# A retention layer's order of work on TensorE and ScalarE: the carried state goes next to the scores, the gate behind the increment, the turning ahead of the output, the output's sum into a gate bank

## The chip, the cores and the metric

The kernel runs on one core of a Trainium2 chip. The metric is the device time of one execution in microseconds. TensorE (PE), VectorE (DVE), ScalarE (ACT) and GpSimd (POOL) each work through a list of instructions of their own, in order, and wait for each other on semaphores. The results of matmuls land in eight PSUM banks of 128 x 512 floats, which DVE and ACT empty.

## What is computed

Two transformer layers on x of 2 x 1024 x 128. Layer 0 is a retention with 8 heads (keys of 64, values of 128), then a feed-forward part that holds a causal attention with 16 heads of 8 and a mixture of four experts. Layer 1 is a full attention with 16 heads and a ternary linear map. The retention, on which the change bears most:

```
q, k = rotary(x Wq), rotary(x Wk);  v = x Wv;  g = x Wg
scores[t, s] = (q_t . k_s) / 8 * gamma_h ** (t - s)   for s <= t
o = groupnorm(scores v) * gn_weight + gn_bias
x = layernorm(x + (o * silu(g)) Wo)
```

## The kernel before

**The retention** (the first quarter of the span) goes over 16 tiles of 128 tokens, 8 for each sequence. In a sequence it runs chunk by chunk: scores inside a tile, and a state of 8 x 64 x 128 that is carried from tile to tile. Everything is in fp32. TensorE's loop over n holds, in this order of issue: the transposes of the turned q and k of tile n (lines 684 and 686, into banks 6 and 7, a wait on `rot_ready` ahead of them), the projection of q and k of tile n+1 (L654, banks 0 and 1), the values of tile n (L705, banks 2 and 3), the scores (L716, banks 4 and 5, which need `qkT_copied` and `onT_affine`), the gate of tile n-1 (`gate_product`, L485, banks 0 and 1, which needs `rot_muls` of tile n+1), the increment of the state (L742, bank 6, needs `v_copied`), the carried state against q (L754, accumulated in banks 2 and 3), the output of the scores (L759, needs `sc_masked`), the projection of tile n-2's gated output (`project_out`, L495, bank 7) and the turning of tile n-1's normed output (`turn_normed`, L504, banks 4 and 5).

Bank 7 has a further use: in tiles 7 to 14 two short pieces a tile of the next stage (latent, q, k, values of the causal attention) pass through it (`use_bank7`, slot 0 ahead of the scores, slot 1 behind the gate; lines 632 to 647).

**ScalarE** in a tile: keeps and squares the output of tile n-1 (`keep_output`, L511 and L514), copies the transposed q and k (L948), applies the group norm's weight and bias to tile n-2 in eight instructions (`affine`, L521), copies the values (L954), opens the gate (`open_gate`, L529). **VectorE**: sums the squares (L535), multiplies for the rotary turn (L786, L787, L789; the last counts `rot_muls`), gates (L542), masks the scores (L812), normalises (L548), adds the state (L826), adds the output to x and takes its statistics (`add_output`, L554 to L557). At the end of tiles 5, 9 and 13 it works out a root and scales four tiles for the next stage (L836, L372 to L376, L440). **GpSimd**: decays the state (L872), works out the root of the group norm (`group_root`, L563, L383 to L387), at tiles 6 and 10 a second root of the same kind (`norm1_rooted`, L432 to L434 and L383 to L387), and turns and scales q and k of tile n+1 (L889, L890, L894; the last counts `rot_ready`).

After tile 15 TensorE goes on along a list that `order()` writes: the gate of tile 15 (D16a), the outputs of tiles 14 and 15 (D16b, D17a) and the first scans. VectorE splits q and k of the second half of sequence 0 (L577) behind the output of tile 13; SyncE stores the parts, loads them back as stacks, and TensorE's first scan (L1519) waits for these.

**The attention of layer 0** has 96 units of 128 keys in 16 blocks. In step s TensorE computes scores (S, L1599 and L1608, two halves x of two heads), scans for a later block's maxima (A, L1519, emptied by VectorE in L1972), and the values of unit s-1 (V, L1634). ScalarE takes the exponentials (L1792), and at the last V of a block it copies the sums out (L1805). In a narrow unit (at most 256 queries) V's half 0 holds no matmul and half 1 holds them all. The lines that set where V stands:

```
for x in range(2):
    if (s, x) in score_use:
        seq.append(("S", (s, x)))
    seq += pairs[...]
    if 0 < s <= NU:
        seq.append(("V", (s - 1, x)))
```

## Time and profile before

| what | value |
|---|---|
| time, median of 3 runs | 996.72 us (996.59 to 1000.06) |
| the profiled execution's own time | 996.77 us |
| its span, first to last instruction | 995.0 us |
| PE busy | 878.4 us (88%) |
| DVE busy | 763.1 us (77%) |
| ACT busy | 654.6 us (66%) |
| POOL busy | 390.0 us (39%) |
| mean granted clock of TensorE | 0.971 |
| chain that ended last | PE 52%, DVE 29%, ACT 7% |

The profile comes from one execution. Starts are in microseconds from the first instruction. A matmul's end is modelled; what a group of matmuls takes is better read as the distance from its start to the start of the group behind it. "T0" below is the start of the q and k transposes of a tile (L684).

### The profile page before, as it was taken

What the parts mean: (1) busy time and instruction counts of PE and PEld (TensorE: products, weight loads), DVE (VectorE), ACT (ScalarE), POOL (GpSimd) and SP (SyncE); (2) the same over time, 40 slices, a digit from 0 to 9 for tenths busy, and PEclk for the clock granted to TensorE, in tenths of its full rate; (3) what the DMA queues carried; (4) which work ended last, traced back from release to release, by engine and by line L of the source; (5) the groups of instructions that cost most, each with busy time, mean ns of one, the idle gap of its engine ahead of it and who ended that gap; (6) DMA issues with size and microseconds to landing.
All of it is one profiled execution on the core that took longest, in us unless ns stands there. A gap on an engine that the chain in (4) does not pass through costs nothing.

```text
span 995.0 us, 22895 instructions
## 1 busy us (share of the span) xinstructions
PE 878.4 (88%) x9093; PEld 446.3 (45%) x9098; DVE 763.1 (77%) x1156; ACT 654.6 (66%) x1285; POOL 390.0 (39%) x607
## 2 busy tenths in 40 slices
PE   8999999998877889888988778889989999999983
PEld 5777777777632443333663222336322222222232
DVE  4677675856587788887567498886889999999845
ACT  3555565655525778785556548765778888998981
POOL 3764767778332652135354111442441111111330
PEclk9999999999899999998998899999999999999995
DMA  8000000200501044111420611033106000100000
GB/s 302 1 2 1 1 2 1 75 1 1 153 1 42 22 132 141 39 41 57 140 63 22 185 23 40 8 111 94 50 13 193 21 20 21 39 2 3 5 22 22
DMA packets 49406, 52.53 MB, mean 53 GB/s; under 512 B 8874, under 2 KB 40618, under 8 KB 49140
## 3 DMA queue, kind: packets, MB, share of 16 engines
q1 hardware_dynamic: 45012, 48.12, 15.9%
q0 software_dynamic: 4288, 2.94, 1.1%
q8 instruction: 73, 1.20, 0.5%
q14 instruction: 33, 0.27, 0.1%
HBM read 32.37 MB, written 19.68 MB: 52 GB/s over the span
## 4 chain that ended last, share of the span: by engine, by line
PE 52%; DVE 29%; ACT 7%; issue 6%; DMA 3%; POOL 2%; SPq 1%; DVEq 0%; ACTq 0%; POOLq 0%
DVE arena L1972 20%; PE banks L1634 11%; PE banks L1599 7%; PE banks L1519 5%; ACT arena L1792 3%; PE banks L759 3%; PE banks L485 3%; PE banks L495 2%; PE banks L1709 2%; PE banks L1717 2%; PE banks L654 1%; PE banks L754 1%; PE banks L716 1%; PE banks L705 1%; ACT arena L521 1%
## 5 line engine op out<-in xcount | busy, mean ns | idle before, releaser
L1792 ACT ACTIVATE arena<-banks 128x512 f32<-128x512 f32 (+1 forms) x768 | 409.3, 587 | 109.2 <-PE banks L1599 78.0
L1972 DVE TENSOR_REDUCE arena<-banks 128x2 f32<-128x1024 f32 (+1 forms) x384 | 439.8, 1197 | 51.9 <-PE banks L1519 27.6
L1634 PE MATMUL banks<-arena 128*9 128x256 f32 (+1 forms) x3328 | 252.1, 378 | 6.7 <-ACT arena L1805 4.6
L1519 PE MATMUL banks<-arena 56*128 56x512 bf16 (+3 forms) x896 | 162.3, 364 | 34.2 <-DVE arena L1972 27.2
L1599 PE MATMUL banks<-arena 61*128 61x512 bf16 (+4 forms) x896 | 164.8, 367 | 26.7 <-ACT arena L1792 21.5
L1599 PEld LDWEIGHTS banks<-arena 61*128 61x128 bf16 (+1 forms) x896 | 44.5, 93 | 183.2 <-ACT arena L1792 155.1
L1376 POOL CAST arena<-arena 16x128 bf16<-16x128 f32 x32 | 8.9, 280 | 293.0 <-ACT arena L1860 289.0
L1634 PEld LDWEIGHTS banks<-arena 128*9 128x9 f32 x3328 | 51.4, 88 | 128.7 <-issue 80.5
L1519 PEld LDWEIGHTS banks<-arena 56*128 56x128 bf16 x896 | 45.0, 95 | 60.7 <-DVE arena L1972 47.8
L383 POOL TENSOR_TENSOR arena<-arena 128x8 f32<-128x8 f32 (+1 forms) x35 | 51.3, 1466 | 30.3 <-DVE arena L2136 27.9
L1386 POOL DMA_DIRECT2D arena<-arena x96 | 55.1, 577 | 10.7 <-POOL arena L1379 9.2
L521 ACT ACTIVATE arena<-banks,arena 128x128 f32<-128x128 f32 x128 | 46.4, 477 | 0.5 <-PE banks L504 0.5
L511 ACT ACTIVATE arena<-banks 128x1024 f32<-128x1024 f32 x16 | 16.4, 1022 | 39.8 <-PE banks L759 39.8
L1969 DVE TENSOR_REDUCE arena<-banks 128x4 f32<-128x1024 f32 (+1 forms) x32 | 30.5, 956 | 14.3 <-PE banks L1529 13.3
L1416 POOL DMA_INDIRECT expert_rows<-arena x22 | 21.3, 970 | 50.9 <-DVE arena L2068 50.6
L554 DVE TENSOR_TENSOR arena<-banks,arena 128x128 f32<-128x128 f32 x16 | 4.6, 290 | 47.0 <-PE banks L495 47.0
L529 ACT ACTIVATE arena<-banks 128x1024 f32<-128x1024 f32 x16 | 16.4, 1026 | 34.2 <-PE banks L485 32.8
L485 PE MATMUL banks<-arena 128*128 128x128 f32 x256 | 34.3, 290 | 2.9 <-DVE arena L789 2.9
L1788 ACT ACTIVATE arena<-banks 128x512 f32<-128x512 f32 (+1 forms) x64 | 27.9, 489 | 13.0 <-PE banks L1608 12.7
L485 PEld LDWEIGHTS banks<-arena 128*128 128x128 f32 x256 | 31.4, 200 | 5.0 <-DVE arena L789 3.0
L759 PE MATMUL banks<-arena 128*128 128x128 f32 x256 | 32.8, 280 | 0.3 <-DVE arena L812 0.3
L495 PE MATMUL banks<-arena 128*128 128x128 f32 x256 | 32.3, 280 | 0.7 <-DVE arena L542 0.7
(243 smaller groups left out, 1442.7 us busy)
## 6 DMA issues: line engine op xcount, KB each, us to landing
arena<-k_products SPq DMA_DIRECT2D x32, 224.0 KB
arena<-q_products SPq DMA_DIRECT2D x64, 112.0 KB
q_products<-arena SPq DMA_DIRECT2D x16, 384.0 KB, 3.4
k_products<-arena SPq DMA_DIRECT2D x16, 384.0 KB, 3.8
arena<-e_w SPq DMA_DIRECT2D x22, 256.0 KB, 3.4
arena<-arena POOLq DMA_DIRECT2D x96, 4.0 KB, 1.8
sorted_rows<-c_pads SPq DMA_DIRECT2D x2, 709.5 KB, 9.3
arena<-sorted_rows SPq DMA_DIRECT2D x4, 258.0 KB, 3.2
```

What stands on the lines that cost most here:

```text
L383: link(eng.tensor_tensor(y, v, epst[:, 1:2].to_broadcast(list(v.shape)), ALU.pow))
L485: ins = nc.tensor.matmul(bank(s // 4)[:, (s % 4) * P:(s % 4 + 1) * P], wg[:, s * P:(s + 1) * P], XT[:, i, :], start=True, stop=True)
L495: ins = nc.tensor.matmul(bank(7)[:, 0:P], uu[:, s, :], wo[:, s, :], start=(s == 0), stop=(s == RH - 1))
L521: ins = nc.scalar.activation(ga[:, s, :], bank(4 + s // 4)[:, (s % 4) * P:(s % 4 + 1) * P], ACT.Identity, scale=gn[:, 0, s:s + 1], bias=gn ...
L759: ins = nc.tensor.matmul(bank(2 + s // 4)[:, (s % 4) * P:(s % 4 + 1) * P], sm[:, s, :], vv[n % 2][:, s, :], start=first, stop=True, skip_g ...
L1386: g_.dma_start(rows, nmp[k % 2][:, i, :]).then_inc(mrow[k % 2], 16)
L1519: ins = nc.tensor.matmul(bank(first + par)[:, at:at + hi - lo], Qs[k_][rows, qc, y, qo:qo + P], Ks[k_][rows, y, lo:hi], start=True, stop=n ...
L1599: ins = nc.tensor.matmul(bank(S_BANK + (use + par) % SCORES)[:, at:at + C - o], Ks[n % NS][rows, y, kt * P:(kt + 1) * P], Qs[n % NS][rows, ...
L1634: ins = nc.tensor.matmul(PS[h * VROWS:h * VROWS + VW, AV_BANK, o:end], V[:, b, kt, HG * g + h, :], Pr[u % PROBS][:, h, o:end], start=(kt = ...
L1792: s_.activation(Pr[s % PROBS][:, 2 * x + par, o:C], scores[:, o:C], ACT.Exp) \
L1969: v_.tensor_reduce(of, two_banks.rearrange("p r (y e) -> p r y e", y=2)[:, :, :, 0:width], AX.X, ALU.max).then_inc(ring_dve, 1)
L1972: v_.tensor_reduce(of[:, :, x], two_banks[:, :, 0:width], AX.X, ALU.max).then_inc(ring_dve, 1)
```

## The change

In the retention, on TensorE: the carried state (L754) moves from behind the increment to right behind the scores, together with the wait on `v_copied`; the increment (L742) follows; the gate (L485) moves behind the increment; the turning (L504) goes ahead of the projection of the output (L495). The sum of that projection is placed in bank 0 for tiles 0 to 13 and in bank 7 for 14 and 15. With this the transposes wait for bank 7's last reader and no longer for `y_added`, the projection of q and k waits for `y_added`, and `project_out` waits for the gate's silu of the tile before (`g_silu`). ScalarE applies the affine (L521) ahead of the copy of the transposed q and k (L948). In `order()` both halves of V follow the first half of the step if the unit is narrow. In D16a the gate of tile 15 waits for `y_added` of tile 13.

```diff
--- before.py
+++ after.py
@@ -486,13 +486,19 @@
                                        wg[:, s * P:(s + 1) * P], XT[:, i, :], start=True, stop=True)
             ins.then_inc(g_done, 1)
 
+        def y_bank(i):
+            return 0 if i < NTILE - 2 else 7
+
         def project_out(pe, i):
 
             pe.wait_ge(u_ready, i + 1)
             ready(pe, y_added, i)
-            ready(pe, use_emptied, sum(at <= (i + 2, 1) for at in USES))
+            if i < NTILE - 2:
+                pe.wait_ge(g_silu, i + 2)
+            else:
+                ready(pe, use_emptied, len(USES))
             for s in range(RH):
-                ins = nc.tensor.matmul(bank(7)[:, 0:P], uu[:, s, :], wo[:, s, :],
+                ins = nc.tensor.matmul(bank(y_bank(i))[:, 0:P], uu[:, s, :], wo[:, s, :],
                                        start=(s == 0), stop=(s == RH - 1))
             ins.then_inc(y_done, 1)
 
@@ -551,7 +557,7 @@
 
             v_ = nc.vector
             dve.wait_ge(y_done, i + 1)
-            v_.tensor_tensor(X[:, i, :], bank(7)[:, 0:P], X[:, i, :], ALU.add).then_inc(y_added, 1)
+            v_.tensor_tensor(X[:, i, :], bank(y_bank(i))[:, 0:P], X[:, i, :], ALU.add).then_inc(y_added, 1)
             dve.wait_ge(y_added, i + 1)
             link(v_.bn_stats(stats[:, i, :], X[:, i, :]))
             link(v_.bn_aggr(mv[:, i, :], stats[:, i, :]))
@@ -678,7 +684,7 @@
                 if this:
 
                     pe.wait_ge(rot_ready, n + 1)
-                    ready(pe, y_added, n - 2)
+                    ready(pe, use_emptied, sum(at <= (n - 1, 1) for at in USES))
                     ready(pe, state_ready, n)
                     for p4 in range(4):
                         nc.tensor.transpose(bank(6)[:, p4 * P:(p4 + 1) * P], qd[n % 2][:, p4 * P:(p4 + 1) * P], ident)
@@ -689,6 +695,7 @@
                 if n + 1 < NTILE and n != 0:
 
                     ready(pe, g_silu, n - 1)
+                    ready(pe, y_added, n - 2)
                     project_qk(n + 1)
                 if n == -1:
 
@@ -716,21 +723,16 @@
                             ins = nc.tensor.matmul(bank(4 + par)[:, p4 * P:(p4 + 1) * P], qkT[rows, 4 + p4, :],
                                                    qkT[rows, p4, :], start=True, stop=True)
                     ins.then_inc(sc_done, 1)
-                i = n - 1
-                if 0 <= i < NTILE:
-
-
-                    if n == 1:
-                        pe.wait_ge(load["gv"], 32)
-                    if n + 1 < NTILE:
-                        pe.wait_ge(rot_muls, n + 2)
-                    else:
-                        pe.wait_ge(g_silu, i)
-                    gate_product(pe, i)
-                use_bank7(n, 1)
+                    pe.wait_ge(v_copied, n + 1)
+                    ready(pe, state_ready, n)
+                    if not first:
+                        for p4 in range(4):
+                            for par in range(2):
+                                rows = slice(par * RD, (par + 1) * RD)
+                                nc.tensor.matmul(bank(2 + par)[:, p4 * P:(p4 + 1) * P], qkT[rows, p4, :],
+                                                 state[(n - 1) % 2][rows, p4 * P:(p4 + 1) * P],
+                                                 start=(p4 == 0), stop=False, skip_group_check=True)
                 if this:
-
-                    pe.wait_ge(v_copied, n + 1)
                     if last:
 
                         nc.tensor.matmul(bank(6)[:, 0:P], ident, ident, start=True, stop=True).then_inc(delta_done, 1)
@@ -744,25 +746,29 @@
                                     kd[n % 2][:, (2 * p4 + par) * RD:(2 * p4 + par + 1) * RD],
                                     vv[n % 2][:, 4 * par + p4, :], start=True, stop=True)
                         ins.then_inc(delta_done, 1)
+                i = n - 1
+                if 0 <= i < NTILE:
+
+
+                    if n == 1:
+                        pe.wait_ge(load["gv"], 32)
+                    if n + 1 < NTILE:
+                        pe.wait_ge(rot_muls, n + 2)
+                    else:
+                        pe.wait_ge(g_silu, i)
+                        pe.wait_ge(y_added, n - 2)
+                    gate_product(pe, i)
+                use_bank7(n, 1)
                 if this:
-
-                    ready(pe, state_ready, n)
-                    if not first:
-                        for p4 in range(4):
-                            for par in range(2):
-                                rows = slice(par * RD, (par + 1) * RD)
-                                nc.tensor.matmul(bank(2 + par)[:, p4 * P:(p4 + 1) * P], qkT[rows, p4, :],
-                                                 state[(n - 1) % 2][rows, p4 * P:(p4 + 1) * P],
-                                                 start=(p4 == 0), stop=False, skip_group_check=True)
                     pe.wait_ge(sc_masked, n + 1)
                     for s in range(RH):
                         ins = nc.tensor.matmul(bank(2 + s // 4)[:, (s % 4) * P:(s % 4 + 1) * P], sm[:, s, :],
                                                vv[n % 2][:, s, :], start=first, stop=True, skip_group_check=not first)
                     ins.then_inc(o_done, 1)
+                if n >= 1:
+                    turn_normed(pe, n - 1)
                 if n >= 2:
                     project_out(pe, n - 2)
-                if n >= 1:
-                    turn_normed(pe, n - 1)
 
         @block.vector
         def _(dve):
@@ -942,12 +948,12 @@
             for n in range(NTILE):
                 if n >= 1:
                     keep_output(act, n - 1)
+                if n >= 2:
+                    affine(act, n - 2)
                 if n < NTILE:
                     act.wait_ge(qkT_done, n + 1)
                     ready(act, o_done, n)
                     s_.activation(qkT.rearrange("p s t -> p (s t)"), pair(3), ACT.Copy).then_inc(qkT_copied, 1)
-                if n >= 2:
-                    affine(act, n - 2)
                 if n < NTILE:
                     act.wait_ge(v_done, n + 1)
                     ready(act, o_done, n - 1)
@@ -1147,7 +1153,8 @@
                     if -6 <= s < 0:
                         seq.append(("warm", 2))
                     if 0 < s <= NU:
-                        seq.append(("V", (s - 1, x)))
+                        late = narrow(*us[s - 1])
+                        seq += [("V", (s - 1, y)) for y in range(2) if (0 if late else y) == x]
                     if x == 0:
                         seq += midst.get(s, [])
                 seq += sorted(after.get(s, []), key=lambda e: (e[0] != "put") + (e[0] == "split"))
@@ -1482,6 +1489,7 @@
                             pe.wait_ge(o_kept if q >= 2 else g_silu, NTILE)
                     if kind == "D16a":
                         pe.wait_ge(g_silu, k)
+                        pe.wait_ge(y_added, k - 1)
                         gate_product(pe, k)
                     elif kind == "D16b":
                         project_out(pe, k - 1)
```

## Rows read from the trace of the kernel before

**Rows 1.** Timeline, tiles 3 and 4: start, us, engine, line, form, count, [idle]

```profile
55.31 1.16 PE L716 MATMUL banks<-arena 64*128 64x128 f32 x16 [0.56 <-ACT arena L521]
56.40 2.05 PE L485 MATMUL banks<-arena 128*128 128x128 f32 x16
...
60.51 2.05 PE L759 MATMUL banks<-arena 128*128 128x128 f32 x16
62.40 1.95 PE L495 MATMUL banks<-arena 128*128 128x128 f32 x16
64.18 1.04 PE L504 MATMUL banks<-arena 128*128 128x128 f32 x8
65.06 0.60 PE L684 MATMUL banks<-arena 128*128 128x128 f32 x4
...
65.93 1.89 PE L654 MATMUL banks<-arena 128*128 128x512 f32 x4
...
67.65 1.88 PE L705 MATMUL banks<-arena 128*128 128x512 f32 x4
...
70.10 1.16 PE L716 MATMUL banks<-arena 64*128 64x128 f32 x16 [0.56 <-ACT arena L521]
...
62.60 1.03 ACT L511 ACTIVATE arena<-banks 128x1024 f32<-128x1024 f32 x1 [3.05 <-PE banks L759]
63.65 1.06 ACT L514 ACTIVATE arena<-arena 128x1024 f32<-128x1024 f32 x1
...
67.05 2.90 ACT L521 ACTIVATE arena<-banks,arena 128x128 f32<-128x128 f32 x8
...
69.79 1.08 ACT L954 ACTIVATE arena<-banks 128x1024 f32<-128x1024 f32 x1
```

**Rows 2.** Timeline, TensorE, the gate of tile 0 in tile 1

```profile
28.39 2.02 PE L485 MATMUL banks<-arena 128*128 128x128 f32 x16 [0.47 <-DVE arena L789]
```

**Rows 3.** Timeline, tile 6: output added, root on GpSimd, tile 7's transposes

```profile
93.96 0.29 DVE L554 TENSOR_TENSOR arena<-banks,arena 128x128 f32<-128x128 f32 x1 [2.38 <-PE banks L495]
...
99.34 0.20 POOL L563 TENSOR_SCALAR arena<-arena 128x8 f32<-128x8 f32 x1 [6.41 <-DVE arena L535]
...
110.03 1.04 POOL L894 TENSOR_TENSOR arena<-arena 128x512 f32<-128x512 f32 x1
...
111.12 0.66 PE L684 MATMUL banks<-arena 128*128 128x128 f32 x4 [0.68 <-POOL arena L894]
```

**Rows 4.** Timeline, end of tile 10: GpSimd's last turn, tile 11's transposes

```profile
172.32 1.04 POOL L894 TENSOR_TENSOR arena<-arena 128x512 f32<-128x512 f32 x1
...
173.65 0.60 PE L684 MATMUL banks<-arena 128*128 128x128 f32 x4
```

**Rows 5.** Timeline, tiles 14 and 15 and the first scan

```profile
228.24 2.05 PE L485 MATMUL banks<-arena 128*128 128x128 f32 x16 [0.83 <-DVE arena L789]
...
237.98 0.60 PE L684 MATMUL banks<-arena 128*128 128x128 f32 x4
...
243.02 1.16 PE L716 MATMUL banks<-arena 64*128 64x128 f32 x16 [2.28 <-ACT arena L521]
...
253.77 1.29 DVE L577 TENSOR_TENSOR arena<-arena 128x512 bf16<-128x512 f32 x2
...
266.71 0.39 PE L1519 MATMUL banks<-arena 56*128 56x512 bf16 x2 [2.06 <-DMA arena<-q_products]
```

**Rows 6.** Stages: length, busy time per engine, granted clock, DMA share, GB/s

```profile
244.00:246.00 2.00, 2.00 (x13) 1.89 (x10) 1.95 (x3) 0.82 (x2) 1.75 (x5) 0.53 0.03 8
246.00:248.00 2.00, 2.00 (x13) 1.88 (x12) 1.18 (x2) 0.18 (x1) 1.47 (x5) 0.62 0.00 0
```

**Rows 7.** Timeline of layer 0's attention, the first step of a block

```profile
401.22 0.39 PE L1599 MATMUL banks<-arena 59*128 59x512 bf16 x2 [0.60 <-ACT arena L1792]
...
401.76 0.41 PE L1634 MATMUL banks<-arena 128*9 128x128 f32 x8
...
402.60 0.61 ACT L1805 ACTIVATE arena<-banks 128x512 f32<-128x512 f32 x1
```

## The prediction

> **What bounds the kernel now.** I read the page's slices first, then the timeline of one plain tile, then the chain that ended last for the places where it leaves TensorE. In the retention TensorE is the bound, and its instructions follow each other with few holes; the reader should look for the holes. A group's length is the distance to the next start. In tile 3 [rows 1] scores take 1.09 (55.31 to 56.40), gate, increment and carried state together 4.11 (to 60.51), the output of the scores 1.89, the projected output 1.78, the turning 0.88, the transposes of q and k 0.87, the projection of q and k 1.72 (65.93 to 67.65); the values, the same shape, another 1.72, to 69.37. Yet the scores start at 70.10. The sum is 14.06, the period 14.79, the hole 0.73 (the row prints 0.56, since ends are modelled). It waits for the affine on ScalarE, which runs 67.05 to 69.95. Tiles 3, 4, 5 and 6 start their scores behind the same hole. In tiles 7 to 14 a piece of the next stage fills it. The other holes: gates that wait for the rotary products (0.47 in tile 1 [rows 2], 0.83 in tile 14 [rows 5]), tile 7's transposes that wait for GpSimd [rows 3], and tile 15, where no projection stands behind the transposes and the hole is 2.28 [rows 5].
>
> **The plain tile after the change.** Count from the start of the transposes, T0. Three lags come from the rows: a consumer starts 0.20 behind the start of the group that follows its producer (62.60 against 62.40), TensorE starts 0.15 behind the end of what it waited for (69.95 to 70.10), and the kept output and its squares take 2.11 (62.60 to 64.71) [rows 1]. The output of the scores now ends at -2.66, ahead of turning and projection. ScalarE keeps it from -2.46 to -0.35, and runs the affine at once, for the turning was done at -1.78: to 2.57. The copy of q and k, taken as long as the values' copy (1.08), ends at 3.65, and TensorE could start the scores at 3.80, while it arrives at 4.31. So that hole is closed, with 0.5 to spare. What is late next is the copy of the values: produced at 4.31, read from 4.51 to 5.59, TensorE may go on at 5.74, but the scores end at 5.40. The gate stood here and hid this; now the carried state waits 0.34. Behind it in TensorE's queue stands all the rest of the tile. I take the whole 0.34; the other bound is a wait of 0.2, if the copy starts TensorE as quickly as the gate of VectorE does. Gain a tile 0.73 - 0.34 = 0.39, for tiles 3, 4 and 5: **1.2**. Moving gate and increment costs nothing here, the sum is the same and the mask is made beside them.
>
> **Tiles 1 and 2.** The wait for the rotary products in tile 1 (0.47 [rows 2]) falls behind carried state and increment; some 0.1 of a wait for the values stays: +0.4. In tile 2 no projected output stands between the scores' output and T0, so ScalarE is late for both orders: 0, between -0.3 and +0.3.
>
> **The output behind the turning is later by a turning.** y is complete 0.88 later against T0: VectorE's `add_output` starts at T0 + 0.20 and no longer at T0 - 0.68. In a plain tile nobody cares. In tile 6 it heads the longest chain of the stage: add (93.96, so T0 is 94.64), root and scaling of four tiles, sum of squares, GpSimd's two roots from 99.34, the turn of q and k to 111.07, tile 7's transposes at 111.12 [rows 3]. This chain takes 17.16 from add to transposes and holds no TensorE work. After the change T0 of tile 7 is 0.20 + 17.16 = 17.36 behind T0 of tile 6; before it was 16.48. **Loss 0.9.** In tile 10 the same chain ended at 173.36 and TensorE came at 173.65 [rows 4], a slack of 0.24 with the lag of 0.05 seen in tile 7: **loss 0.88 - 0.24 = 0.6.** The adds of tile 5's and 9's last step can't hide it: TensorE's own work in tile 6 comes to at most 15.5, so it stands idle 1.9 ahead of T0 of tile 7. Tile 14 has no second root; its gate's 0.83 goes and nothing is late in its place: **gain 0.8.** In the other tiles the order of equal parts changes and the hole isn't there: 0, between -0.3 and +0.3 in all.
>
> **Tile 15.** Before: T0 at 237.98, scores at 243.02, L577 at 253.77 [rows 5], 15.79 behind T0. In these 15.79 the granted clock fell from 2.4 to 1.2 GHz after the hole: 0.53 and 0.62 of full in two stretches of 2 us [rows 6], which is 2 x 0.47 + 2 x 0.38 = 1.7 us of work lost. After: transposes and values to 2.59; the copy of q and k lets the scores start at 3.80 (a hole of 1.2); scores and carried state 2.2, an identity product in the increment's place 0.3, the gate 2.0: 8.3; output of the scores 1.9, turning 0.9, projected output 1.8: 12.9; add at 13.1, its statistics 0.87 as before: L577 at about 13.9. **Gain 1.9**, of which the late output took 0.9. From L577 the way goes over SyncE and DMAs to the first scan at 266.71, which waited for them 2.06 [rows 5]; nothing of the change lies in it. TensorE's other work there has that 2 us of slack against 0.4 us in which it now starts later relative to L577, and the gate of tile 15, which waits 0.6 for the add of tile 13, has the same cover. So what L577 gains the scans gain.
>
> **The clock.** The new idle 1.9 ahead of tile 7 is a new risk. Holes of 0.6 to 0.8 left the clock at 2.4 GHz all through the stage; 2.28 was followed by 1.2 GHz [rows 5, 6]. 1.9 is nearer to the second, and VectorE's mask already holds TensorE about 1 us before it. I take one fall, at the price above: **loss 1.7**, between 0 and 3.4 (tile 11's transposes wait 1.4 as well). The Trainium skill, "TensorE: Matmul & The Clock Gate", section "Part 4: PE-mode transpose", says that a transpose doesn't count as busy for that gate; by this the 0.87 of transposes behind each wait counts as idle too, and both tiles would lose the clock. The trace of before neither shows nor denies it.
>
> **Layer 0's narrow values.** A narrow unit's values move only where something stood between the halves. That is the last unit of a block, sixteen times: its V (0.41, rows 7) passes ahead of the second half's scores, its A, and a block's end. Exponentials wait there at present: TensorE stood 0.60 for ScalarE before the second scores [rows 7], and V now fills that. Up to 0.41 a block, 6.6 in all, if TensorE sets the pace after it, but VectorE's scans or ScalarE do in most steps, and ScalarE has the same instructions: its copy out (0.61) only goes ahead of two exponentials. I take a gain of **0.5**, between -3 and +4.
>
> **Sum.** 1.2 + 0.4 - 0.9 - 0.6 + 0.8 + 1.9 = 2.8 in the retention, less 1.7 for the clock, plus 0.5: 1.6 off the profiled execution's 996.77 (span 995.0, with 1.8 around it), which is within 0.1 of the median. **995.2 us.**
>
> **Rivals.**
> - *The clock holds.* For it: 1.9 us is shorter than any hole after which it fell. 996.8 - 2.8 - 0.5 = 993.5. If V's move is worth 3 more in bubbles, 990.5.
> - *Both of GpSimd's waits cost the clock,* tiles 7 and 11: 996.8 - 2.8 + 3.4 - 0.5 = 996.9. For it the rule on transposes, which the sentence above names; against it 1.4 us of idle is much shorter than 2.28.
> - *Slower: the copy out blocks ScalarE.* It now stands ahead of the second half's exponentials and waits for V, which stands behind the first scan, and so behind VectorE. If VectorE is late there, ScalarE stands with scores ready. Price: the copy's 0.61 once more in each of 16 blocks, 9.8, against the 1.1 that is left: 1005. It decides where ScalarE is the bound and VectorE behind. Against it: the second scores stood behind the same scan before, and the copy had to be over before the next block's V anyway.
> - *The copy of values isn't hidden in more tiles than thought,* or the sum in bank 0 makes the projection wait for the add: 0.28 us of slack in a plain tile. 0.3 in ten tiles would be 3: 998.
>
> **How the numbers follow.** Forecast 0.38; clock holds 0.27; both clocks 0.13; more waits 0.09; slower by the copy 0.07; a large gain in layer 0 0.06. A measurement can tell about 0.5% (5 us). Faster by that, below 991.8, needs the clock and layer 0 together: 0.18. Slower, above 1001.7, needs the copy or several of the waits: 0.09. Same 0.73. Range 989.5 to 1000.0.
>
> **What would show it.** Right: plain tiles 14.4 apart; no wait of L716 for L521, and one of about 0.3 of L754 for L954; T0 of tile 7 17.4 behind T0 of tile 6 with GpSimd as releaser; L577 13.9 behind T0 of tile 15, and TensorE at full clock between. Wrong: a period of 14.06 or over 14.8; tile 7 on time; L1805 with idle time ahead of it on ScalarE in each block; the granted clock at half in tiles other than 7. The prediction fails above all if the falls of the clock in the attention, whose places move with every microsecond, change in number.

## The result and the profile after

The changed kernel takes 990.4 us (median of 8 runs, 987.9 to 992.4) where the kernel before takes 996.7 in the same rounds (8 runs, 994.1 to 1000.1): a ratio of 0.9923, 95% interval 0.9903 to 0.9943. In later rounds, beside the experiments, it was 992.5 against 997.4, ratio 0.9947 (0.9923 to 0.9970). So it is faster by 5 to 6 us. The forecast was 995.2, a gain of 1.6: the time lies inside the range of 989.5 to 1000.0, but the gain is some four times what the sum gave, and it is the "faster, below 991.8" to which the prediction gave 0.18.

The profiled execution took 990.96 us, its span is 989.2 (before: 995.0). From here on "T0" is the start of the transposes of q and k (L690 now, L684 before), and a tile's length is the distance to the next T0. Lines have moved: scores are L723, carried state L732, increment L744, output of the scores L765, projected output L501, turning L510, affine L527, copy of q and k L956, copy of the values L960.

| stretch | before, us | after, us | difference | forecast |
|---|---|---|---|---|
| start to T0 of tile 1 | 22.35 | 22.15 | -0.20 | 0 |
| tiles 1 and 2 | 27.92 | 26.84 | -1.08 | -0.4 |
| tiles 3, 4 and 5, together | 44.36 | 42.16 | -2.20 | -1.2 |
| tile 6 | 16.49 | 17.37 | +0.88 | +0.9 |
| tiles 7, 8 and 9 | 45.55 | 44.37 | -1.18 | 0, and +1.7 for the clock |
| tile 10 | 16.98 | 17.83 | +0.85 | +0.6 |
| tiles 11, 12 and 13 | 47.34 | 46.78 | -0.56 | 0 |
| tile 14 | 16.99 | 15.93 | -1.06 | -0.8 |
| T0 of tile 15 to the first scan | 28.73 | 26.32 | -2.41 | -1.9 |
| first scan at | 266.71 | 259.75 | -6.96 | -1.1 |
| first scan to the end of the span | 728.3 | 729.45 | +1.2 | -0.5 |

Timeline of the kernel after, tile 3 on TensorE and ScalarE (start, us, engine, line, form, count, idle before), the lines that answer to [rows 1]:

```profile
51.59 1.88 PE L712 MATMUL banks<-arena 128*128 128x512 f32 x4
53.40 1.16 PE L723 MATMUL banks<-arena 64*128 64x128 f32 x16
54.59 1.16 PE L732 MATMUL banks<-arena 64*128 64x128 f32 x16
55.68 1.10 PE L744 MATMUL banks<-arena 128*64 128x128 f32 x16
56.71 2.05 PE L485 MATMUL banks<-arena 128*128 128x128 f32 x16
58.60 1.95 PE L765 MATMUL banks<-arena 128*128 128x128 f32 x16
60.38 1.04 PE L510 MATMUL banks<-arena 128*128 128x128 f32 x8
61.26 1.95 PE L501 MATMUL banks<-arena 128*128 128x128 f32 x16
63.05 0.60 PE L690 MATMUL banks<-arena 128*128 128x128 f32 x4
...
48.55 2.88 ACT L527 ACTIVATE arena<-banks,arena 128x128 f32<-128x128 f32 x8
51.28 1.06 ACT L956 ACTIVATE arena<-banks 128x1024 f32<-128x1024 f32 x1
53.51 1.02 ACT L960 ACTIVATE arena<-banks 128x1024 f32<-128x1024 f32 x1 [1.16 <-PE banks L712]
```

The scores stand right behind the values (51.59 to 53.40) and no longer behind a hole: the copy of q and k ends at 52.34, a microsecond ahead of them. The carried state starts at 54.59, 0.06 behind the end of the copy of the values (53.51 + 1.02), so it does wait for it, though no idle time is printed.

Timeline of the kernel after, tiles 6 and 10: the add of the output and the transposes at the other end of the chain, the lines that answer to [rows 3] and [rows 4]:

```profile
91.35 0.29 DVE L560 TENSOR_TENSOR arena<-banks,arena 128x128 f32<-128x128 f32 x1 [2.47 <-PE banks L501]
...
108.52 0.66 PE L690 MATMUL banks<-arena 128*128 128x128 f32 x4 [1.78 <-POOL arena L900]
...
170.72 0.66 PE L690 MATMUL banks<-arena 128*128 128x128 f32 x4 [1.72 <-POOL arena L900]
```

From add to transposes it is 108.52 - 91.35 = 17.17 us in tile 6, and TensorE stands idle 1.78 and 1.72 us ahead of tiles 7 and 11.

Timeline of the kernel after, tile 15 and the first scan, the lines that answer to [rows 5] (SPq is SyncE's queue of transfers), and the stretches behind T0 of tiles 7 and 15 (length, busy time per engine, granted clock, DMA share, GB/s), which answer to [rows 6]:

```profile
233.43 0.60 PE L690 MATMUL banks<-arena 128*128 128x128 f32 x4
...
236.84 1.16 PE L723 MATMUL banks<-arena 64*128 64x128 f32 x16 [0.65 <-ACT arena L956]
...
246.97 1.29 DVE L583 TENSOR_TENSOR arena<-arena 128x512 bf16<-128x512 f32 x2
...
254.68 0.78 SPq L1248 DMA_DIRECT2D arena<-k_products  x2
...
259.75 0.39 PE L1527 MATMUL banks<-arena 56*128 56x512 bf16 x2 [1.35 <-DMA arena<-q_products]
...
108.00:110.00 2.00, 1.48 (x10) 1.24 (x11) 1.22 (x1) 2.00 (x6) 1.88 (x3) 1.00 0.00 0
...
244.00:246.00 2.00, 2.00 (x19) 1.87 (x17) 0.00 (x0) 1.97 (x3) 1.67 (x5) 1.00 0.02 4
```

The granted clock is 1.00 (2.4 GHz) in every such stretch, behind both waits for GpSimd as in tile 15. VectorE's part splitting L583 (the L577 of before) stands 13.54 behind T0 of tile 15, where it stood 15.79.

### The profile page after: what moved, and what is told of

Its sections match the earlier page's. It is cut to its first block, busy times and chain, and to the rows that moved or that the text cites. A ratio compares the mean times of both kernels' runs of the same rounds, so it can differ in the third digit from the quotient of the medians.

```text
span 989.2 us, 22910 instructions
## 1 busy us (share of the span) xinstructions
PE 877.2 (89%) x9098; PEld 440.9 (45%) x9098; DVE 764.4 (77%) x1156; ACT 652.9 (66%) x1285; POOL 390.4 (39%) x607
## 4 chain that ended last, share of the span: by engine, by line
PE 41%; DVE 27%; POOL 12%; issue 9%; ACT 6%; DMA 3%; SPq 2%; DVEq 0%; POOLq 0%; ACTq 0%
DVE arena L1980 19%; PE banks L1642 11%; PE banks L1607 7%; PE banks L1527 5%; ACT arena L1800 4%; POOL arena L383 2%; PE banks L1717 2%; PE banks L1725 2%; DMA arena<-arena 1%; PE banks L660 1%; POOL arena L896 1%; POOL arena L895 1%; PE banks L501 1%; PE banks L765 1%; POOL arena L386 1%
## 5 line engine op out<-in xcount | busy, mean ns | idle before, releaser
L1642 PE MATMUL banks<-arena 128*9 128x256 f32 (+1 forms) x3328 | 254.8, 382 | 5.8 <-ACT arena L1813 3.9
L535 ACT ACTIVATE arena<-banks 128x1024 f32<-128x1024 f32 x16 | 16.4, 1024 | 56.9 <-PE banks L485 55.5
L527 ACT ACTIVATE arena<-banks,arena 128x128 f32<-128x128 f32 x128 | 46.1, 466 | 0.0
L501 PE MATMUL banks<-arena 128*128 128x128 f32 x256 | 31.4, 275 | 2.0 <-DVE arena L548 2.0
L485 PE MATMUL banks<-arena 128*128 128x128 f32 x256 | 32.6, 281 | 0.6 <-DVE arena L560 0.5
L765 PE MATMUL banks<-arena 128*128 128x128 f32 x256 | 31.9, 277 | 1.2 <-DVE arena L818 1.2
L765 PEld LDWEIGHTS banks<-arena 128*128 128x128 f32 x256 | 30.0, 191 | 4.4 <-issue 2.5
L501 PEld LDWEIGHTS banks<-arena 128*128 128x128 f32 x256 | 29.8, 191 | 3.0 <-DVE arena L548 3.0
```

Of the source, the lines that this page charges most:

```text
L485: ins = nc.tensor.matmul(bank(s // 4)[:, (s % 4) * P:(s % 4 + 1) * P], wg[:, s * P:(s + 1) * P], XT[:, i, :], start=True, stop=True)
L501: ins = nc.tensor.matmul(bank(y_bank(i))[:, 0:P], uu[:, s, :], wo[:, s, :], start=(s == 0), stop=(s == RH - 1))
L527: ins = nc.scalar.activation(ga[:, s, :], bank(4 + s // 4)[:, (s % 4) * P:(s % 4 + 1) * P], ACT.Identity, scale=gn[:, 0, s:s + 1], bias=gn ...
L765: ins = nc.tensor.matmul(bank(2 + s // 4)[:, (s % 4) * P:(s % 4 + 1) * P], sm[:, s, :], vv[n % 2][:, s, :], start=first, stop=True, skip_g ...
L1642: ins = nc.tensor.matmul(PS[h * VROWS:h * VROWS + VW, AV_BANK, o:end], V[:, b, kt, HG * g + h, :], Pr[u % PROBS][:, h, o:end], start=(kt = ...
```

## Experiments

"Before" and "after" name the two kernels. Times are medians with the ratio to before and its 95% interval, measured in the same rounds.

### The two parts apart

`e1_values_only` is before with the new order of V alone, `e2_retention_only` is after with the old one:

```diff
-                        late = narrow(*us[s - 1])
-                        seq += [("V", (s - 1, y)) for y in range(2) if (0 if late else y) == x]
+                        seq.append(("V", (s - 1, x)))
```

> The kernel before with layer 0's narrow values alone moved (the order of work in the attention), the retention as it was. The two whole kernels stand 0.77% apart; the traces put 7.0 us of it ahead of the first scan. Theory 1 (the retention holds all of it, the values are worth the 0.5 us of the prediction): ratio 0.9995, between 0.998 and 1.001. Rival (the values fill TensorE's bubbles at each block's end and carry 2 us or more): 0.998 or below. Rival (the copy out blocks ScalarE): above 1.002.

> The changed kernel with the attention's order put back: only the retention's edits. Theory 1: the first scan starts at 259.8 as in the changed kernel, ratio about 0.993. If the values carried 2 us or more, the ratio is 0.995 or above.

Measured: e1 997.2 us, ratio 0.9985 (0.9964 to 1.0007); e2 992.6 us, ratio 0.9929 (0.9900 to 0.9958). The whole gain that can be measured is the retention's. Its tiles in e2 are those of after within 0.03 us, and its first scan stands at T0 of tile 15 + 26.57.

What V's order does is seen in layer 0's first block. Timeline of e1, ScalarE, the exponentials (L1793), the copy out (L1806) and the copy behind it (L1861):

```profile
306.22 0.61 ACT L1806 ACTIVATE arena<-banks 128x512 f32<-128x512 f32 x1
306.69 1.11 ACT L1793 ACTIVATE arena<-banks 128x512 f32<-128x512 f32 x2
307.65 0.25 ACT L1861 ACTIVATE arena<-banks 16x128 f32<-16x128 f32 x1
```

In before the copy out stands at 307.82 and L1860, which is this kernel's L1861, at 308.30. So the copy out is 1.6 earlier, but 1.0 of that is only its new place ahead of two exponentials; the work itself is 0.65 earlier. By L1860/L1861 the lead grows to 0.84 at 343, 1.05 at 375, 1.38 at 421 and 1.9 at 464: some 0.1 to 0.2 a block, no idle time ahead of the copy. So the slower rival (the copy out blocks ScalarE) is out. By the copy that starts at 641.66 in e1 and 646.21 in before the lead is 4.6 in these two profiles, but e1's is its fastest run; between e2 and after at the same place it is nothing (640.66 and 640.72), though e2's first scan is 0.9 later. Two runs further down, e10 and e8, ask the same of whole times once more.

### The turning behind the output again

`e3_output_first` is after with the projected output ahead of the turning, its sum still in bank 0:

```diff
+                if n >= 2:
+                    project_out(pe, n - 2)
                 if n >= 1:
                     turn_normed(pe, n - 1)
-                if n >= 2:
-                    project_out(pe, n - 2)
```

> The changed kernel with the projected output again ahead of the turning, its sum still in bank 0. Theory (the output behind the turning is late by one turning, 0.88 us, at the head of the chains of tiles 6, 10 and 15): the transposes of tile 7 come 16.5 behind those of tile 6 (17.37 in the changed kernel), those of tile 11 16.9 to 17.0 behind those of tile 10 (17.83), the first scan 0.9 earlier against the transposes of tile 15; plain tiles stay at 14.05, since the affine has 0.5 us to spare. In all 2.6 us less than the changed kernel, ratio 0.990 to 0.991. Rival (the affine, now started by a turning that is 1.79 later, holds the scores again): plain tiles at 14.3 to 14.8 and no gain over the changed kernel.

Measured: 987.5 us, ratio 0.9877 (0.9843 to 0.9911). Plain tiles stay at 14.05, tile 6 takes 16.51, tile 10 17.15. So the late output costs what the prediction put on it, 0.86 and 0.68, and gives nothing back: closing the hole doesn't need it. Timeline of e3, part splitting, the first load of a stack and the first scan:

```profile
245.30 1.29 DVE L583 TENSOR_TENSOR arena<-arena 128x512 bf16<-128x512 f32 x2
...
253.01 0.78 SPq L1248 DMA_DIRECT2D arena<-k_products  x2
...
259.89 0.39 PE L1527 MATMUL banks<-arena 56*128 56x512 bf16 x2 [3.70 <-DMA arena<-q_products]
```

L583 comes 12.83 behind T0 of tile 15 (after: 13.54), and the load starts 7.71 behind it in both. But the loads then took 6.88 us to the scan, where after's took 5.07: the scan stands no earlier than in after in this profile.

### ScalarE's old order

`e4_copy_first` is after with ScalarE's copy of q and k ahead of the affine, as in before:

```diff
                 if n >= 1:
                     keep_output(act, n - 1)
-                if n >= 2:
-                    affine(act, n - 2)
                 if n < NTILE:
                     act.wait_ge(qkT_done, n + 1)
...
+                if n >= 2:
+                    affine(act, n - 2)
```

> The changed kernel with ScalarE's copy of the transposed q and k again ahead of the affine. Theory (the hole before the scores was ScalarE's order alone, and the turning's place would not have closed it): the scores of tiles 3 to 6 wait for the affine again, 0.6 to 0.75 a tile, plain tiles at 14.6 to 14.8, tile 15's scores wait over 2 us and the clock falls to half behind it; the gain before the first scan shrinks from 7.0 to 1 to 3 us. Rival (the earlier turning lets the affine start early enough in any order): plain tiles at 14.05.

Measured: 993.3 us, ratio 0.9942 (0.9917 to 0.9967), and its first scan is at 265.18; 2.1 of the 5.4 by which that is later than after's lie in a later start and a longer tile 0, ahead of all that the edit touches. Timeline of e4, tile 5 on TensorE, from its T0 to the next, and the scores of tile 15:

```profile
79.89 0.60 PE L690 MATMUL banks<-arena 128*128 128x128 f32 x4
...
84.92 1.16 PE L723 MATMUL banks<-arena 64*128 64x128 f32 x16 [0.55 <-ACT arena L527]
85.88 1.09 PE L732 MATMUL banks<-arena 64*128 64x128 f32 x16
...
94.27 0.60 PE L690 MATMUL banks<-arena 128*128 128x128 f32 x4
...
241.38 1.16 PE L723 MATMUL banks<-arena 64*128 64x128 f32 x16 [2.27 <-ACT arena L527]
```

The hole is back (0.55, as in [rows 1]), yet a plain tile takes 14.38, not 14.6 to 14.8. The scores start 5.03 behind T0, as before; the 9.35 from there to the next T0 were 9.75 in before (55.31 to 65.06, [rows 1]). The difference of 0.4 is TensorE's own order. In after the same stretch takes 9.65 (53.40 to 63.05), though TensorE's order is that of e4: so the wait for the copy of the values, which is over in time in e4, costs after 0.30. Of this 0.23 shows in the scores (1.19 against 0.96) and the rest in the carried state behind them. In tile 15 the wait for the affine is back too (2.27), the clock falls to half behind it, and L583 stands 16.24 behind T0 where after has 13.54. So of what after gained up to L583, ScalarE's order holds the larger part: 1.7 us between T0 of tile 0 and T0 of tile 15, and 2.7 behind it.

### The length of the wait and the clock

`e5_longer_wait` is after with three products more on GpSimd ahead of the root of tile 6:

```diff
                         pool.wait_ge(n1_scaled, m + 1)
+                        if m == 0:
+                            for _ in range(3):
+                                link(g_.tensor_tensor(sq, ident, ident, ALU.mult))
                         norm1_rooted(link, m).then_inc(n1_rooted, 1)
```

> The changed kernel with three products more on GpSimd (128x128 each) ahead of its root in tile 6, so that TensorE's wait ahead of tile 7's transposes grows from 1.78 us to about 2.8; the rest is the same. Theory A (the length of the idle time decides whether TensorE's clock falls: 1.78 left it at full, 2.06 and 2.28 in the kernel before did not): the granted clock falls behind T0(7), tile 7 grows from 14.34 by 1.5 to 2 us, the first scan comes 1.0 + 1.7 = 2.7 later at about 262.5, and the time is 2.5 to 3 us above the changed kernel's 990.4: 993. Rival B (transposes behind the wait and the place in the stage matter, not its length: tile 15's hole is special): the clock stays at full, tile 7 stays 14.34, the first scan comes 1.0 later at 260.8, the time is 991.4.

Timeline of e5, T0 of tiles 7 and 8, and the stretch behind the first:

```profile
110.36 1.11 PE L690 MATMUL banks<-arena 128*128 128x128 f32 x4 [3.17 <-POOL arena L903]
...
126.35 0.60 PE L690 MATMUL banks<-arena 128*128 128x128 f32 x4
...
110.00:112.00 2.00, 1.64 (x8) 1.64 (x9) 1.22 (x1) 2.00 (x7) 1.78 (x4) 0.59 0.00 0
```

Measured: the wait is 3.17 instead of 1.78 (tile 6 grows by 1.39, where 1.0 was expected), the clock falls to half behind it (0.59 of full in the first stretch, 0.56 in the next), and tile 7 takes 15.99 instead of 14.34, 1.65 more. Theory A held in this place: the wait was short enough in after, and the price of a fall that I had put on it (1.7) is the right one. The time is 994.0, ratio 0.9934 (0.9904 to 0.9963); its interval overlaps after's, so the 3 us rest on the profile.

`e6_filled_hole` is before with nine idle products where TensorE stood still in tile 15; their results are used by nobody:

```diff
                     ins.then_inc(v_done, 1)
+                    if n == NTILE - 1:
+                        pe.wait_ge(g_silu, n - 1)
+                        for _ in range(9):
+                            nc.tensor.matmul(bank(0)[:, 0:P], ident, ident, start=True, stop=True)
```

> The kernel before with nine fp32 products of the identity into an unused bank, queued behind tile 15's projections, where TensorE stands idle for 2.28 us; nothing else is changed, and the results of the nine are used by nobody. Theory A (the fall of the clock behind this hole costs 1.7 us of tile 15): scores still start at T0(15) + 5.0, the granted clock is full in 244 to 248, L577 for the last parts comes 1.7 earlier at T0(15) + 14.1 and the first scan 1.7 earlier, at 265.0. Rival B (the fall costs nothing, as the way to L577 goes through ScalarE and VectorE): L577 stays at T0(15) + 15.8 and the scan at 266.7. Rival C (the clock falls in spite of the filling): granted clock 0.5 to 0.6 as before.

Timeline of e6, tile 15 to the first scan, and its stretch of the clock:

```profile
240.96 2.17 PE L711 MATMUL banks<-arena 128*128 128x128 f32 x18
243.40 1.16 PE L720 MATMUL banks<-arena 64*128 64x128 f32 x16 [0.27 <-ACT arena L521]
...
252.53 1.29 DVE L577 TENSOR_TENSOR arena<-arena 128x512 bf16<-128x512 f32 x2
...
266.39 0.39 PE L1523 MATMUL banks<-arena 56*128 56x512 bf16 x2 [2.98 <-DMA arena<-q_products]
...
244.00:246.00 2.00, 2.00 (x24) 1.88 (x21) 1.91 (x3) 1.20 (x3) 1.67 (x6) 1.00 0.04 8
```

Measured: T0 is at 238.37, the scores start 5.03 behind it as before, the clock stays full, and L577 stands 14.16 behind T0 instead of 15.79. The fall of the clock had cost 1.63 there. Of this only 0.71 reached the first scan (28.02 behind T0, before 28.73), for the way from L577 to the scan took 13.86 instead of 12.94. In the whole time no gain can be told: 998.1 us, ratio 0.9990 (0.9964 to 1.0017).

### The gate's place

`e7_gate_between` is after with the gate back behind the scores, ahead of the carried state and the increment. The short piece of the next stage that follows the gate in tiles 7 to 14 (`use_bank7`, slot 1) moves with it; the rest is as in after:

```diff
                     ins.then_inc(sc_done, 1)
+                i = n - 1
+                if 0 <= i < NTILE:
...
+                    gate_product(pe, i)
+                use_bank7(n, 1)
+                if this:
                     pe.wait_ge(v_copied, n + 1)
                     ready(pe, state_ready, n)
...
-                    gate_product(pe, i)
-                use_bank7(n, 1)
```

> The changed kernel with the gate back between the scores and the carried state; the increment stays behind the carried state. It hides the copy of the values again. Theory A (prediction's term: the copy of the values is waited for; measured only 0.1 in the changed kernel, while the other 0.2 of the gain comes from joins, groups of 16 products being 0.1 shorter behind a group of full tiles): the wait of 0.1 goes, the gate takes 1.98 behind the scores in place of 1.89, and the output of the scores 1.89 behind the increment in place of 1.78: plain tiles come to 14.05 - 0.1 + 0.2 = 14.15. Rival B (joins are worth nothing): 13.95. Rival C (the wait is in truth larger and hidden): 13.7. In tiles 7, 9, 11 and 13 theory A gives back part of the 0.4 to 0.6 that they lost: +0.1 to +0.3 each. Time: 991.5 by A, 989 by B.

Timeline of e7, TensorE in tile 4, then the gates of tiles 6 and 14, and the clock behind the first of these:

```profile
68.93 1.16 PE L723 MATMUL banks<-arena 64*128 64x128 f32 x16
70.03 2.05 PE L485 MATMUL banks<-arena 128*128 128x128 f32 x16
72.01 1.16 PE L746 MATMUL banks<-arena 64*128 64x128 f32 x16
73.10 1.10 PE L758 MATMUL banks<-arena 128*64 128x128 f32 x16
74.13 2.05 PE L766 MATMUL banks<-arena 128*128 128x128 f32 x16
...
100.70 3.31 PE L485 MATMUL banks<-arena 128*128 128x128 f32 x16 [2.30 <-DVE arena L796]
...
229.34 2.05 PE L485 MATMUL banks<-arena 128*128 128x128 f32 x16 [1.91 <-DVE arena L796]
...
102.00:104.00 2.00, 2.00 (x12) 1.77 (x11) 2.00 (x3) 0.00 (x0) 1.67 (x6) 0.50 0.00 0
```

Measured: plain tiles 14.15, as theory A had it. Its number is right and its two parts are not: it took 0.1 for the wait that goes and 0.2 for the groups that get longer, and by e4 they are 0.30 and 0.40, with the same difference. Nothing waits in tile 4, and it is 0.1 longer than after's, which does wait: gate and output take 1.98 and 1.89 here, 1.89 and 1.78 in after. But more came to light: this kernel reaches T0 of tile 15 223.46 us behind T0 of tile 0, after in 218.42, before in 222.77. Of these 5.0 us, 1.94 are in tile 14, 0.74 in tile 6, 0.62 in tile 1: the gate stands in TensorE's queue ahead of work that is ready, and waits for the rotary products of VectorE (2.30, 1.91). Behind the 2.30 the clock falls to half as well. With every hole of the affine closed, no gain over before can be told in whole times: 995.5 us, ratio 1.0001 (0.9966 to 1.0036). Six of its ten runs took 992.7 to 996.1 and four 1002.7 to 1004.6, and the profile is of the fastest, so the 5.0 us rest on the profile. No size was expected for this.

The gate's place isn't alone in these waits. In before the gate of tile 6 waited too, by less:

```profile
101.63 2.05 PE L485 MATMUL banks<-arena 128*128 128x128 f32 x16 [0.80 <-DVE arena L789]
```

That is 7.00 behind T0, in e7 7.87; in tiles 10 and 14 it is 7.25 in before and 8.33 in e7. VectorE's rotary products stand behind the add of the output in its queue, and the add comes 0.87 later against T0 since the output goes behind the turning. So some 0.9 of each of these three waits belongs to the late output. The gate in its old place with the output ahead of the turning was not run.

### GpSimd's rotation ahead of its root

`e9_rotation_first` is e3 with the root of tiles 6 and 10 behind the rotation:

```diff
                 for m in range(3):
-                    if n == first_of(m) - (m < 2):
+                    if m == 2 and n == first_of(m):
                         pool.wait_ge(n1_scaled, m + 1)
...
                     ins.then_inc(rot_ready, 1)
+                for m in range(2):
+                    if n == first_of(m) - 1:
+                        pool.wait_ge(n1_scaled, m + 1)
+                        norm1_rooted(link, m).then_inc(n1_rooted, 1)
```

> The projected output ahead of the turning (as in e3_output_first), and GpSimd's rotation for tiles 7 and 11 ahead of its root of the norm in tiles 6 and 10. What is left of idle time there is GpSimd's queue: 1.8 us ahead of tile 7 and 1.7 ahead of tile 11 in the changed kernel. If the root's users (norm, then the first piece in bank 7 of the tile that follows) still come in time, T0(7) - T0(6) falls from 16.5 to about 15.2 and T0(11) - T0(10) from 17.15 to about 15.8: 2.6 us less than e3_output_first's 987.5, 984.9. Rival: the root is late for the piece in bank 7, which stands in TensorE's queue ahead of the scores: tiles 7 and 11 grow by as much as tiles 6 and 10 shrink, 987.5.

Timeline of e9, the wait in tile 7 on TensorE and ScalarE, the same wait in tile 11, and the clock behind each:

```profile
118.57 0.63 PE L638 MATMUL banks<-arena 128*128 128x128 f32 x4 [2.85 <-issue]
...
111.50 1.28 ACT L447 ACTIVATE arena<-arena 128x128 f32<-128x128 f32 x4 [5.59 <-POOL arena L387]
...
183.07 1.11 PE L638 MATMUL banks<-arena 128*128 128x128 f32 x4 [2.80 <-ACT arena L960]
...
118.00:120.00 2.00, 1.43 (x18) 1.29 (x20) 1.97 (x3) 1.99 (x3) 1.76 (x4) 1.00 0.03 8
...
184.00:186.00 2.00, 2.00 (x19) 1.89 (x20) 0.76 (x1) 1.72 (x3) 1.83 (x4) 0.50 0.03 8
```

Measured: tiles 6 and 10 shrink to 14.55 and 15.90 (15.2 and 15.8 were expected), but tiles 7 and 11 grow to 18.94 and 22.24: 995.5 us, ratio 0.9982 (0.9952 to 1.0012). The rival won, and by more than it asked; tile 11 lost the clock besides (0.50). What it had missed is ScalarE: its product with the root (L447) stands ahead of everything of tile 7 in ScalarE's queue, waits 5.59 for GpSimd, and the output of tile 6, the affine and the copy of q and k stand behind it.

### Both orders again, on one chip

`e10_output_first_again` is the code of e3, `e11_changed_again` that of after, and `e8_output_first_old_values` is e3 with V in its old order (the diff of e2).

> The same kernel as e3_output_first (projected output ahead of the turning, its sum in bank 0), on the same chip and in the same rounds as the changed kernel (e11) and as the version with the old order of the values (e8). Theory: the retention up to L583 of tile 15 is 1.7 us shorter than in the changed kernel (245.30 against 246.97), since the late output costs 0.87 in tiles 6 and 0.68 in tile 10 and 0.7 in tile 15 (13.54 against 12.83), less small start differences; how much of it reaches the first scan depends on the transfers (5.07 or 6.88 us from the first load to the scan). Expected 988.5 where the changed kernel has 990.4, ratio 0.990 to before. Rival: the 987.5 was luck in where the clock falls in the attention; then the same as e11 within 1 us.

> The changed kernel itself, as a yardstick in these rounds: 990 to 992, ratio 0.992 to 0.994 to before.

> Output ahead of the turning, and layer 0's values in their old order. Theory A (the order of the values is worth 1 to 2 us: first copy out 39.2 to 39.4 us behind the first scan with it, 41.1 to 41.5 without, and part of it is given back before the end): 1 to 2 us above e10. Rival B (all of it is given back, as e1_values_only's ratio of 0.9985 allows): the same as e10. In the profile: first copy out 41.3 behind the first scan.

Measured: e10 988.4 us, ratio 0.9890 (0.9866 to 0.9914); e11 992.5, ratio 0.9947 (0.9923 to 0.9970); e8 987.4, ratio 0.9894 (0.9873 to 0.9915). So output ahead of turning is faster than the changed kernel by some 4 us, with intervals that don't touch, and it beats both kernels. Timeline of e10, part splitting and first scan:

```profile
245.60 1.29 DVE L583 TENSOR_TENSOR arena<-arena 128x512 bf16<-128x512 f32 x2
...
258.63 0.39 PE L1527 MATMUL banks<-arena 56*128 56x512 bf16 x2 [2.14 <-DMA arena<-q_products]
```

The scan follows L583 by 13.03 here, as in after (12.78) and before (12.94); e3's 14.59 was an exception, as was e6's 13.86. T0 of tile 0 to L583 takes 229.72, in after 231.96: 2.2 of the 4 us lie there, the rest was not placed. Rival B of e8 holds: the order of the values is worth nothing in the whole time. In its profile it is worth something for a while: at 359.41 against 358.71 and 458.92 against 457.34 (L1867 and L1868), but at the copies of 612.75 and 614.00 e8 is ahead.

## Why the prediction was right and wrong

**Right.** *What closes and what is late next:* the hole of the plain tile went, and the copy of the values is waited for. *The late output:* 17.36 was forecast from T0 of tile 6 to T0 of tile 7, 17.37 measured; tile 10 lost 0.85 for 0.6. e3 confirms the cause: 0.86 and 0.68 come back with the old order. *Tile 14:* a gain of 1.06 for 0.8. *Tile 15:* L583 13.54 behind T0 for 13.9, and all of it reached the scan; of the 2.25 gained, e6 shows 1.63 as the clock's, and e3 shows 0.71 that the late output still costs. *The values:* no price on ScalarE.

**Luck.** The measured 990.4 is what the rival "the clock holds" had at its far end (990.5), with the values' move worth 3 more. The clock held, but the values' move is worth nothing in whole times; the rest came from the retention, by the steps below.

**Wrong: the clock (1.7 us).** The step that failed is "1.9 is nearer to the second. I take one fall". The wait came out at 1.78, as worked out, and the clock did not fall; the term was worth 0. e5 shows that the price was right and where it would have been due: a wait of 3.17 in the same place cost 1.65. The rival "the clock holds" had the outcome, but its ground, that 1.9 is shorter than any hole after which the clock fell, isn't so in the trace of before. Its retention holds no wait between 0.83 and 2.28, and in its attention a wait of 1.79 was followed by half clock (one of 1.13, at 465.52, too):

```profile
521.72 0.38 PE L1571 MATMUL banks<-arena 128*16 128x128 f32 x1 [1.79 <-DVE arena L1972]
...
521.00:523.00 2.00, 1.07 (x5) 0.30 (x5) 1.80 (x2) 0.53 (x2) 1.86 (x2) 0.50 0.00 0
```

So before could not decide between the two; it took a run of the change. The Trainium skill, "TensorE: Matmul & The Clock Gate", section "Part 4: PE-mode transpose", says that a transpose doesn't count as busy in the same way as other matmuls; by that 1.78 of waiting and 0.93 of transposes would be 2.7 of idleness, above the 2.28 that cost the clock in before. The trace doesn't bear that out: the clock stayed at full in tile 7 and tile 11 of after.

**Wrong: the plain tile (1.0 us in three tiles, and more elsewhere).** The sum gave 14.4, the kernel does 14.05; the prediction had named 14.06 as a sign of being wrong. The step that failed is "Moving gate and increment costs nothing here, the sum is the same": a group of eight products (x16 in the rows) has no length of its own. The gate takes 1.98 behind the scores and 1.89 behind the increment; the output of the scores 1.89 behind carried state or increment and 1.78 behind the gate; the scores 1.10 ahead of the gate and 0.96 to 1.00 ahead of the carried state. By e4 the new order is 0.40 shorter. The values take 1.81 right ahead of the scores and not 1.72; they do so in before too (24.94 to 26.75 in tile 1), so its hole was 0.64 and not 0.73. The wait for the values, taken at 0.34, was nearly right: 0.30. This gives 14.06 + 0.09 - 0.40 + 0.30 = 14.05. e7 takes the 0.40 away again, and the wait with it: 14.15.

**Wrong: tiles 7 to 9 and 11 to 13 (1.7 us).** They stood at 0 because the hole isn't printed there. They gained 0.2 to 0.6 each (tile 12 lost 0.32, where a piece in bank 7 waits 0.44 for the copy of q and k). e7 is longer than after by 0.28, 0.19 and 0.01 in tiles 7, 8 and 9 and by 0.31, 0.25 and 0.01 in 11, 12 and 13, which is the place of the gate and of the piece behind it; what the rest is made of was not taken apart.

**Wrong: tiles 1 and 2 (0.7 us).** They gained 0.62 and 0.46 instead of 0.4 and 0. e7 gives back 0.62 and 0.36 of it: it is the gate's place.

**The gate was looked at least.** The prediction costed its move through two waits (0.47 and 0.83) and at nothing elsewhere. The same wait stood in tiles 6 and 10 of before as well (0.80 and 0.82), where the chain over GpSimd hid all or most of it; the prediction's list of holes doesn't have them. By e7 the gate's place is worth 5.0 us up to T0 of tile 15, with the rest of the change in place, the late output included. Closing the holes by ScalarE's order and setting the output behind the turning both lengthen its wait for VectorE, if it stays where it was.

**Layer 0.** 0.5 was forecast for the values, and 0 is measured in whole times (e1: 0.9985, e8 against e10). Within the first eleven blocks the profiles show 1.6 to 1.9 us. By 646 nothing of them is left between e8 and e10 or between e2 and after; between e1 and before the 4.6 there hold other differences too. Before, after and e11 lose the clock at different places between 440 and 640: after shows 0.83, 0.83 and 0.89 in the stretches of ten microseconds from 590, 610 and 630, before shows 1.00 in all three. That fits the 2.5 us that after's lead loses there (7.9 at the copy that starts at 588.38 in before and 580.44 in after, 5.5 at the copy out of 646), but no run moved these falls alone, so it is argued and not shown. From there to the end both kernels go at one pace: of the 7.0 us at the first scan, 5.8 are left in the span.

## What to carry to other kernels

When a queue's hole is closed by making another engine earlier, list what each in-order queue waits for next, and put the piece whose producer is latest last among equals; here that was the gate, which waited 2.30 and 1.91 us in its old place. Take a group's length from a row in which the same neighbours stand around it, and price a wait over the whole stretch up to the next common point, for one row holds only a part of it. Look for a wait's like in the whole trace, not in the stage alone. When a change bundles moves, price each as if it stood alone: one of them (the turning ahead of the output) cost some 4 us, of which 2.2 could be placed, and bought nothing.

## What the runs showed of the hardware

- The length of an idle spell decides mostly, and not alone, whether TensorE's clock falls. In the retention single waits of 1.31, 1.58, 1.72, 1.78 and 1.91 us were followed by 2.4 GHz; 2.27, 2.28, 2.30 and 3.17 by 1.2 GHz within 2 us. Ahead of the first scan 1.99, 2.06, 2.08, 2.14, 2.29, 2.98 and 3.70 were followed by 1.2 GHz too. There are exceptions both ways: e9's 2.85 left the clock at full while its 2.80 cost it; ahead of the first scan, where other short waits precede, 1.50 (e11), 1.56 (e2) and 1.69 (e5, e7) were followed by half clock and 1.35 (after) was not; and in the attention of before 1.13 and 1.79 were followed by half clock. The Trainium skill, "TensorE: Matmul & The Clock Gate", Part 1, says of the clock's rise at a kernel's start that it comes at different points in different runs of the same kernel; after and e11, which are the same code, show such a difference in a fall.
- A group of eight fp32 products of 128 x 128, which the profile counts as x16, took between 1.78 and 1.98 us at full clock, by its neighbours alone.
- The same loads of the first stack took 4.9 to 5.5 us from first issue to the scan in eleven profiles, 6.17 in e6 and 6.88 in e3. What delayed them was not found.
